# A decoder layer on one core: every step of the five queues set at a new place

## The reference

```python
# 1: x = LN(x + attn(x)); keys and values are weights
xn = LN(x) * ln_g + ln_b                      # 4 heads of 64
p = square(relu(einsum(xn, k)))               # k: 1024 x 64
y = x + einsum(p, v)
# 2: x = LN(x + xattn(x, ctx)); 16 heads of 16
attn = gamma * q @ k.T / 4 + delta * (ap * max(D, 0) + an * min(D, 0))
probs = softmax(attn); out = (probs @ v) @ Wo.T + bo     # D = clip(frac_k - frac_q)
# 3: x = LN(x + ffn(x)); the best of 8 experts by x @ gate_W.T + gate_b
inter = relu(x @ wi.T + wi_b + low_rank(expert)); out = inter @ wo.T + wo_b
```

## Time and profile before

| | us |
|---|---|
| median of 3 runs | 862.24 (862.21 to 862.75) |
| the profiled execution | 863.64 |
| its span, first to last instruction | 861.6 |
| PE busy | 827.0 (96%) |
| ACT busy | 698.4 (81%) |
| DVE busy | 679.7 (79%) |
| POOL busy | 599.0 (70%) |
| DMA queue q1, share of 16 engines | 26.1% |
| mean granted TensorE clock | 0.989 |

### The profile page before, as it was taken

One profiled execution on the slowest core, in us unless ns is written; L12 is line 12 of the kernel. 1 busy time (PEld: TensorE's weight loads), 2 busy tenths in 40 slices (PEclk: granted clock), 3 DMA queues, 4 the chain that ended last, 5 costly groups with the idle time before them and its releaser, 6 DMA issues.

```text
span 861.6 us, 23381 instructions
## 1 busy us (share of the span) xinstructions
PE 827.0 (96%) x8444; PEld 596.2 (69%) x8444; DVE 679.7 (79%) x2104; ACT 698.4 (81%) x1930; POOL 599.0 (70%) x782
## 2 busy tenths in 40 slices
PE   8989999999999999999999999999999999999897
PEld 6555557767676776767677676767767676677676
DVE  6788897878788787888878788787878877798943
ACT  4569998897988889798888979888897988887841
POOL 6478897777868687786868778686877867552411
PEclk9999999999999999999999999999999999999998
DMA  6242323222222322221232223123222312313100
GB/s 178 75 91 60 60 48 59 48 39 43 55 46 58 54 64 39 56 57 32 62 56 57 38 57 61 27 65 54 56 38 47 71 29 49 56 33 56 32 14 25
DMA packets 38149, 46.32 MB, mean 54 GB/s; under 512 B 10417, under 2 KB 27313, under 8 KB 38034
## 3 DMA queue, kind: packets, MB, share of 16 engines
q1 hardware_dynamic: 38034, 44.82, 26.1%
HBM read 15.42 MB, written 4.19 MB: 23 GB/s over the span
## 4 chain that ended last, share of the span: by engine, by line
PE 83%; ACT 7%; DVE 7%; issue 2%; POOL 1%; SPq 0%; DMA 0%; POOLq 0%; DVEq 0%; ACTq 0%
PE bank L308 12%; PE bank L295 12%; PE bank L503 11%; PE bank L256 10%; PE bank L421 8%; PE bank L435 6%; PE bank L405 4%; PE bank L381 4%; ACT R L655 2%; PE bank L328 2%; PE bank L362 2%; ACT P L711 2%; PE bank L342 2%; DVE T L940 2%; PE bank L513 2%
## 5 line engine op out<-in xcount | busy, mean ns | idle before, releaser
L1163 POOL TENSOR_TENSOR R<-R 128x512 f32<-128x512 f32 x236 | 247.3, 1050 | 84.9 <-ACT R L655 84.6
L711 ACT ACTIVATE P<-T,NM 128x256 f32<-128x256 f32 x512 | 257.5, 515 | 2.9 <-DVE NM L940 2.9
L1181 POOL TENSOR_SCALAR U<-DP,alph 128x512 f32<-128x512 f32 x256 | 180.3, 705 | 112.9 <-DVE NM L940 79.8
L931 DVE SCALAR_TENSOR_TENSOR bank<-DN,alph,bank 128x512 f32<-128x512 f32 x256 | 179.7, 747 | 53.5 <-PE bank L405 53.3
L940 DVE CUSTOM_DVE_ANT_0 T<-bank,U 128x256 f32<-128x256 f32 x512 | 186.4, 420 | 1.5 <-issue 0.6
L655 ACT ACTIVATE R<-bank 128x512 f32<-128x512 f32 x248 | 134.9, 601 | 61.8 <-PE bank L295 55.5
L633 ACT ACTIVATE STG<-bank 128x512 f32<-128x512 f32 x256 | 138.8, 600 | 8.5 <-PE bank L421 7.9
L308 PE MATMUL bank<-R,VS 128*32 128x512 f32 x992 | 120.6, 602 | 1.1 <-DVE X2b L884 0.9
L295 PE MATMUL bank<-SK,KH 64*128 64x512 f32 x480 | 108.5, 448 | 4.2 <-ACT R L655 1.4
L711 ACT ACTIVATION_READ_ACCUMULATOR P<-T,NM 128x1 f32 x512 | 105.5, 206 | 0.0
L421 PEld LDWEIGHTS bank<-ident,P 64*128 64x128 f32 x2048 | 75.4, 139 | 36.7 <-issue 13.6
(11 more groups left out here) (178 smaller groups left out, 1769.0 us busy)
## 6 DMA issues: line engine op xcount, KB each, us to landing
QS<-QK SPq DMA_DIRECT2D x384, 64.0 KB, 2.3
XG<-in_x SPq DMA_DIRECT2D x16, 256.0 KB, 2.8
CT<-in_ctxT SPq DMA_DIRECT2D x16, 256.0 KB, 3.2
out<-XO SPq DMA_DIRECT2D x15, 256.0 KB, 2.5
FK<-in_frac SPq DMA_DIRECT2D x16, 128.0 KB, 3.1
STG<-in_wiT SPq DMA_DIRECT2D x2, 512.0 KB, 4.4
STG<-in_woT SPq DMA_DIRECT2D x2, 512.0 KB, 4.4
STG<-in_kT SPq DMA_DIRECT2D x2, 256.0 KB, 4.1
```

The costliest lines, as they stand in the source:

```text
L711: eng.activation(P[n % NP][:, cs], T[n % NT][:, cs], ACT.Exp, bias=NM[:, n % 8, q:q + 1], scale=-1.0, accum_out=SU[n // 16 % 2][:, q, seat ...
L931: eng.scalar_tensor_tensor(out=L[:, :], in0=dn[:, :], scalar=alph[:, 16 + h:17 + h], in1=L[:, :], op0=ALU.mult, op1=ALU.add).then_inc(s_t1, 1)
L1163: eng.tensor_tensor(r, r, r, ALU.mult).then_inc(s_sqp, 1)
L1181: eng.tensor_scalar(U[n % NU][:, :], dp[:, :], alph[:, h:h + 1], 0.0, ALU.mult, ALU.add).then_inc(s_u, 1)
```

## The change

The functions that make the steps are not touched. What changes is the numbers at which the five GRID loops issue them: all `due` lines and all `g ==` lines, except a few. No step is added, dropped or given another operand; buffers and waits are written as before. Since `take` runs in the order of PE's queue, the banks of some steps change, and with them the step whose reader they wait for.

```diff
             for g in GRID:
-                if g == -4898:
+                if g == -3786:
                     pe.wait_ge(s_id, 1)
                     filler(15, pV)
...
-                for b, u in due(g, -4, 8, 74, early=27):
+                for b, u in due(g, 6, 8, 72, early=33, late=11):
                     logits(8 * b + u)
-                for b, u in due(g, 1308, 4, 33, early=-8, late=164):
+                for b, u in due(g, 1312, 4, 31, early=-16, late=118):
                     ffn_in(b, u)
-                for b, u in due(g, 1311, 4, 32, early=-8, late=227):
+                for b, u in due(g, 1320, 4, 29, early=-14, late=173):
                     low_rank(b, u)
-                for b, u in due(g, 1434, 8, 23, early=1, late=1136):
+                for b, u in due(g, 1432, 8, 24, late=1751):
                     ffn_out(b, u)
-                for b, _ in due(g, 767, early=-36, late=-21):
+                for b, _ in due(g, 767, early=-42, late=1):
                     rcT(b)
-                for b, u in due(g, 121, 8, 78, early=39, late=15):
+                for b, u in due(g, 121, 8, 78, early=50, late=40):
                     turn(8 * b + u)
-                for b, u in due(g, -946, 4, 151, early=-105):
+                for b, u in due(g, -951, 4, 154, early=4, late=-2):
                     av(b, u)
-                for b, u in due(g, 276, 4, 149, early=37, late=52):
+                for b, u in due(g, 276, 4, 147, early=29, late=63):
                     values(4 * b + u)
...
-                for b, _ in due(g, 861, early=45, late=-10):
+                for b, _ in due(g, 880, early=-13, late=-63):
                     op(b)
-                if g == -1061:
+                if g == -724:
                     bias_o()
-                for b, _ in due(g, -253, late=-8):
+                for b, _ in due(g, -264, early=-84, late=-2):
                     turned_over("x1T", b, X1, s_x1, 2 * b + 2, s_x1T)
-                for b, _ in due(g, -231, early=-900, late=37):
+                for b, _ in due(g, -220, early=-498, late=29):
                     kp(b)
...
-                for b, _ in due(g, 1236, early=-24, late=227):
+                for b, _ in due(g, 1265, early=5, late=190):
                     gsT(b)
-                for b, _ in due(g, 1289, early=-9, late=243):
+                for b, _ in due(g, 1308, early=-30, late=183):
                     uT(b)
-                for b, u in due(g, -1151, 8, 73, early=-255, late=4):
+                for b, u in due(g, -1151, 8, 73, early=-156, late=2):
                     scores(b, u)
...
-                for b, _ in due(g, 825, early=-7, late=103):
+                for b, _ in due(g, 771, early=-19, late=49):
                     aoh(b)
...
-                for b, _ in due(g, 681, early=-28, late=-104):
+                for b, _ in due(g, 570, early=68, late=139):
                     rc(b)
...
-                for b, _ in due(g, 2023, early=77, late=1318):
+                for b, _ in due(g, 2018, early=10, late=1718):
                     dve.wait_ge(d_o, 16 * b)
...
-                for b, u in due(g, 405, 4, 92, early=187, late=-230):
+                for b, u in due(g, 1090, 4, 56, early=-83, late=431):
                     restack(4 * b + u)
-                for b, _ in due(g, 2, start=1, late=-225):
+                for b, _ in due(g, 460, start=1, late=474):
                     load_f(b)
...
-                for b, _ in due(g, 2686, early=425, late=1586):
+                for b, _ in due(g, 3663, early=58, late=-615):
                     if b == NB - 1:
```

More of the change, by code:

```diff
@@ L604, in _ @@
                     turned_over("x1T", b, X1, s_x1, 2 * b + 2, s_x1T)
-                for b, _ in due(g, -231, early=-900, late=37):
+                for b, _ in due(g, -220, early=-498, late=29):
                     kp(b)
-                for b, _ in due(g, -208, early=18, late=29):
+                for b, _ in due(g, -216, early=12, late=52):
                     qp(b)
-                for b, _ in due(g, -138, early=128, late=-24):
+                for b, _ in due(g, -140, early=69, late=-17):
@@ L610, in _ @@
                     vp(b)
-                for b, _ in due(g, 1112, early=20, late=294):
+                for b, _ in due(g, 1121, early=13, late=85):
                     turned_over("x2T", b, X2, s_x2, 2 * b + 2, s_x2T)
-                for b, _ in due(g, 1163, early=14, late=300):
+                for b, _ in due(g, 1184, early=-32, late=209):
                     gate(b)
-                for b, _ in due(g, 1236, early=-24, late=227):
+                for b, _ in due(g, 1265, early=5, late=190):
@@ L624, in _ @@
                     xnT(1)
-                for b, _ in due(g, -1220, start=2, late=-2):
+                for b, _ in due(g, -1218, start=2, late=-15):
                     xnT(b)
@@ L767, in _ @@
             for g in GRID:
-                for b, u in due(g, 1289, 4, 36, early=-4, late=1653):
+                for b, u in due(g, 1301, 4, 31, early=-7, late=1544):
                     ih(b, u)
-                for b, _ in due(g, -374, early=-541):
+                for b, _ in due(g, -399, early=-2597, late=1):
                     x1(b)
-                for b, u in due(g, 29, 16, 37, early=20, late=21):
+                for b, u in due(g, 29, 16, 37, early=24, late=19):
                     exps(16 * b + u)
-                if g == -4264:
+                if g == -3916:
@@ L775, in _ @@
                     skh(0)
-                if g == -1560:
+                if g == -1133:
                     skh(1)
-                for b, _ in due(g, -1268, start=2, late=11):
+                for b, _ in due(g, -1259, start=2, late=4):
                     skh(b)
-                for b, _ in due(g, -498, early=-164, late=13):
+                for b, _ in due(g, -505, early=55, late=-8):
                     heads_out(b)
-                for b, u in due(g, 114, 8, 76, early=35, late=52):
+                for b, u in due(g, 111, 8, 78, early=31, late=60):
@@ L830, in _ @@
                     gs(b)
-                for b, _ in due(g, 1285, early=-43, late=-39):
+                for b, _ in due(g, 1273, early=-35, late=445):
                     ulh(b)
-                for b, u in due(g, -1160, 8, 70, early=-1041, late=6):
+                for b, u in due(g, -1155, 8, 69, early=-1077, late=6):
                     relu(b, 2 * u)
@@ L1079, in _ @@
                         centred("d", b, XO, X2b, s_xo)
-                if g == -2096:
+                if g == -1667:
                     dve.wait_ge(d_small, 160)
@@ L1116, in _ @@
                     cl(b)
-                for b, _ in due(g, -235, early=-14, late=64):
+                for b, _ in due(g, -268, early=-70, late=61):
                     low("x1T", b, X1L, X1H, s_x1h, s_x1l)
-                for b, _ in due(g, -206, early=-1396, late=77):
+                for b, _ in due(g, -240, early=-1260, late=59):
                     projected("kp", b, 2, 2, s_kh, s_kl)
-                for b, _ in due(g, -178, early=-22, late=58):
+                for b, _ in due(g, -205, early=17, late=59):
@@ L1122, in _ @@
                     projected("qp", b, 1, 0, s_qh, s_ql)
-                for b, _ in due(g, 1164, early=-41, late=-91):
+                for b, _ in due(g, 1145, early=-48, late=226):
                     low("x2T", b, X2L, X2H, s_x2h, s_x2l)
-                for b, _ in due(g, 1193, early=18, late=540):
+                for b, _ in due(g, 1196, early=-25, late=285):
                     gating(b)
-                for b, _ in due(g, 1282, early=15, late=961):
+                for b, _ in due(g, 1254, early=20, late=1376):
@@ L1128, in _ @@
                     ull(b)
-                for b, u in due(g, -1309, 16, 50, early=-674, late=107):
+                for b, u in due(g, -1213, 16, 43, early=-797, late=840):
                     if on_dve(b, u):
@@ L1225, in _ @@
                     plus(X1b[b % 2], X1, boB, s_x1b)
-                for b, _ in due(g, 1546, early=-342, late=131):
+                for b, _ in due(g, 1396, early=-61, late=260):
                     pool.wait_ge(s_x2, 2 * b + 2)
@@ L1231, in _ @@
                     plus(X2b, X2, woB, s_x2b)
-                for b, u in due(g, -1057, 16, 40, early=-591):
+                for b, u in due(g, -1112, 16, 36, early=-269, late=23):
                     if not on_dve(b, u):
```

200 lines of the change are left out of this document (100 added, 100 removed).

## The result

| | before | after |
|---|---|---|
| median of 18 runs each, us | 862.73 (860.43 to 864.40) | 856.90 (854.47 to 861.98) |
| ratio after to before, 95% interval | | 0.9934 (0.9921 to 0.9947) |
| the profiled execution | 863.64 | 857.19 |
| its span | 861.6 | 855.3 |
| mean granted TensorE clock | 0.989 | 0.990 |

The account below looks back on a forecast made before the run. TensorE was taken to bound the middle, ScalarE the ramp, latency the start, VectorE then latency the tail. From 863.64 us, block 4.8, head 3.9 and tail 1.8 gave 853.1, less 1.40 to the median: 851.7; range 846 to 859.

Parts of the forecast that it names:

- (a): TensorE, end of each steady block: logits 0 behind scores 7 and uT behind turn 7 gain 0.49 us a block.
- a wait on `exps` at `turn` 7: Sign of a wrong forecast, at the end of a steady block on TensorE; no size given.
- The wait that was to come back at `ffn_in`: End of each block: part of turn 7's wait returns at ffn_in 0, listed at 0.2 to 0.3 us in 12 blocks.
- (b): Steady block on TensorE: logits 7 ahead of turn 5 loses 0.06 us a block.
- (c): TensorE: values 3 ahead of logits 1, ffn_out 3 ahead of op; swaps booked at nothing, 0.03 us lost for the second.
- (d): Steady-block moves on the other engines, such as rc ahead of ull; each has 0.4 us or more to spare.
- The order of steps has a price: Steady block: TensorE loses time between one kind of step and the next, priced by distances between starts.
- Part 2: Head: x1T 5.2 us earlier, a quarter of the gain let go, first logits at 55.3, so 3.9 us gained.
- later than 58: Sign of a wrong forecast: logits 0 in the head starting after 58 us, where 55 to 56 was expected.
- rival B: Ramp: ScalarE, full from 100 to 150 us, swallows the head's gain; 855.6 us, chance 0.22.
- Part 3: Tail, from 750 us: low_rank's 1.05 us wait for ull goes and op 15 comes earlier; 1.8 us gained.
- Rival E: SyncE's queue: restack 1 behind load_f and the out DMA loses 6 us in 13 blocks; 940 us, chance 0.03.

Follow-up runs that it names:

- e5_noc: Kernel after with logits 1 ahead of values 3 again in the middle blocks; 858.28 us (one run).
- e7_rc: Kernel before with logits 0 behind scores 7, uT behind turn 7, values 3 ahead of logits 1, rc ahead of ull; 858.21 us (one run).
- e4_head: Kernel after with the first half-block's y1 ahead of the weights on VectorE; 854.97 us, ratio to before 0.9911.
- e10_head: Kernel before with only the head of the kernel after (steps due below 300 moved); 862.61 us, ratio to before 1.0008.
- e6_head: Kernel after with turn 5 ahead of logits 7, y1 ahead of the weights, and the way to the first logits cleared; 853.52 us, ratio to before 0.9898.
- e1_ut: Kernel before with only uT moved behind turn 7; 859.47 us (one run).
- e1_a: Kernel before with logits 0 of blocks 2 to 14 behind scores 7 and uT behind turn 7; 861.39 us, ratio to before 0.9988.
- e8_best: Kernel after with y1 ahead of the weights, turn 5 ahead of logits 7, and block 1's first logits ahead of scores 7; 853.07 us, ratio to before 0.9887.
- e3_nob: Kernel after with turn 5 ahead of logits 7 again in all blocks but first and last; 855.85 us, ratio to before 0.9912.

## Why the prediction was right, and where it was not

- **What bounds the middle, and (a) at `ffn_in` 0: right.** 4.65 became 4.19 (4.16 forecast). Its pieces too: `gsT` to `av` 0.20 (0.17), `scores` to `logits` 0.23 (0.24), `turn` 0.65 (0.64), `logits` to `turn` 0.41 where 0.34 was forecast. That 0.07 reads as a short wait for `exps`, by the 0.14 us that `turn` 7 keeps behind its end in each block; a wait on `exps` at `turn` 7 was one of my signs of being wrong, and it came, small. The wait that was to come back at `ffn_in` is there, as 0.28 from `uT` in place of 0.15, bound by the `relu` as forecast, but too short for the list of waits, where I had said it would show.
- **(b): right.** 0.07 against 0.06 us.
- **(c) and (d), "I book nothing" and "each has 0.4 us or more": wrong.** I compared each swap with its two neighbours on TensorE under the old timing. But (a) sends `uT` back and with it VectorE's chain from `ull` on, which ends at `logits` 1 and at `scores` 0. The swap of `values` 3 is worth 0.21 (e5_noc), `rc` ahead of `ull` 0.22 (e7_rc against e1_ac). Without them (a) gives 0.19, and with them 0.46. The change had both, and it also had (b) at 0.07 and some 0.06 that are left against e7_rc: 0.46 - 0.07 - 0.06 = 0.33, where 0.40 was forecast. The size came near for a wrong reason.
- **The order of steps has a price: right, but it is small.** If it were free, a block with the wait of 0.37 gone would take 49.64. e7_rc, with no wait listed, takes 49.55, so the new order is 0.09 us shorter. The formula N/2.4 + 2.5 ns between starts at the full clock, which the Trainium skill gives on its page TensorE: Matmul & The Clock Gate (Back-to-back issue gap), has no term for the neighbour, but the page keeps it to an isolated matmul and says that in a stream the weight load sets the spacing too. So it is no word for a free order, and no run here tells the weight load's part.
- **Part 2, the head: wrong in two steps.** First, `x1T` was to come 5.2 sooner: 3 from `otT`, and "all but 0.6" of the open 2.8 us ahead of `x1T`. `otT` came 2.2 sooner (38.20 and 36.04). The open 2.8 went, but 3.2 came on VectorE where 0.6 was allowed: `y1` started 2.45 us behind the end of `otT` (39.12 and 36.67), as the two weights ahead of it took 2.06 us each where they took 1.22 before, and `centred` b took 1.49 and not 0.74. e4_head confirms it: with `y1` ahead of them `x1T` comes at 42.70 although its `otT` was 1.2 later. Second, and decisive, the gain was to pass through the ramp, less a quarter. It does not (e10_head: 0.9 us at `logits` 0 at most, none in the time; e6_head: 3.1 us there, 0.9 at the next). The first `logits` at 59.11 also met a sign of being wrong, "later than 58". That was rival B, to which I gave 0.22, and its 855.6 is nearer to 856.9 than my 851.7. Its argument, that ScalarE is full from 100 to 150 and what starts sooner "only queues sooner", is not shown: most of the gain of e6_head is gone at `logits` 1, at 62 us already, and what holds the ramp, ScalarE, VectorE or another, was not tested.
- **Part 3, the tail: right in size, by luck in part.** 2.1 us in the profile against 1.8, and the wait of `low_rank` went as said, with 0.68 of its 0.95 us left at `op` 15. But the same steps behind `gsT` 12 take 119.6 us in the kernel after, with 13.7 us at the lower level of the clock, and 117.1 in e4_head, with 6.8. Against the 121.7 us of the kernel before that is a gain of 2.1 or of 4.5, by the profile that is taken.
- **Rival E: out.** No wait for QS in the middle of either profile.

## What to carry to other kernels

When a queue is bound by one engine, price a swap by the new timing, not the old: list every step that the main edit delays on the other engines, follow each to the next place where the bound engine waits for it, and see whether one of the "free" swaps stands there. Test the main edit alone and in halves; here one half was better than the whole. A head start at one milestone is not a gain: follow a second milestone, one step of work further, before it enters the sum.

## What the runs showed of the hardware

**The clock of TensorE moves the time by as much as the edits do.** The traces show two levels, 2.4 GHz (granted 1.00) and 1.2 GHz (0.50), and spells at the lower one that fall differently in each kernel, all ahead of 110 us and behind 770. There TensorE has idle gaps: it is busy for some 44 of 50 us from 60 to 110 in the kernels of the table of the head, 87.32 of 100 in the last row below. The columns are those of the earlier trace rows; first the kernel before, then the kernel after, then e1_ut, which has no such spell in the tail:

```profile
64.50:67.90 3.40, 3.40 (x21) 0.74 (x18) 3.12 (x10) 2.06 (x6) 3.40 (x4) 0.58 0.63 98
```

```profile
807.90:818.10 10.20, 9.15 (x85) 5.73 (x78) 6.30 (x26) 7.53 (x24) 2.31 (x4) 0.53 0.01 2
```

```profile
750.00:850.00 100.00, 87.32 (x924) 73.33 (x923) 76.19 (x241) 66.30 (x194) 34.00 (x53) 1.00 0.16 32
```

From `gsT` 12 to the end the kernel before, with 10.2 us at the lower level, takes 121.7 us, and e1_ut, whose tail differs by the place of `uT` alone, takes 119.2 with none: 2.5 us. In the 18 runs of the kernel after the span is 852.6 to 854.6 where the mean clock was 0.993 or 0.994, 855.0 to 856.6 at 0.990 to 0.992, and 860.0 at 0.986. In e1_a the mean clock was 0.988 to 0.990 in all ten runs, beside 0.989 to 0.994 in the kernel before: its middle is some 2.1 us shorter (11 times 0.19), its time only 0.8. In its profile `gsT` 1 comes at 187.64, 1.3 us later than before, with two spells between 60 and 110 us where before has one. So a new order can also bring or take such spells, and a few tenths of a per cent of the time say nothing without the clock beside them.

**VectorE and GpSimd hold each other up.** The subtraction of a weight (128x1024) on VectorE occurs 56 times in the fourteen profiles. The 40 that began while GpSimd was idle took 1.21 to 1.23 us, also where GpSimd started during them. Sixteen began inside an instruction of GpSimd. Fourteen of these took as long as was left of GpSimd's instruction, and 1.07 to 1.09 us more: 2.05 or 2.06 with 0.98 left, 1.75 with 0.66 left (e8_best), 1.46 with 0.38 left (e3_nob). The other two took 1.21 and 1.22; there GpSimd's instruction, of a kind that takes 1.05 on the mean, took 2.12 (e4_head) and 2.94 (e3_nob), so it looks as if GpSimd was the one held up. Here are the two GpSimd instructions inside which the weights at 35.15 and 37.13 of the kernel after began:

```profile
35.00 1.13 POOL L1163 TENSOR_TENSOR R<-R 128x512 f32<-128x512 f32 x1 [6.86 <-ACT R L655]
...
36.78 1.33 POOL L1163 TENSOR_TENSOR R<-R 128x512 f32<-128x512 f32 x1 [0.65 <-ACT R L655]
```

The Trainium skill says on its page SBUF — State Buffer (Terms, shared port pair) that the two share a pair of ports which is locked for a whole instruction, and that the loser blocks fully. Blocked until GpSimd's end (36.13 and 38.11) the two would end at 37.35 and 39.33; they end at 37.21 and 39.19, 0.14 sooner. So the rows agree with a block much more than with a shared speed. In the kernel before the same weights happened to meet an idle GpSimd; the difference, 1.7 us for the two, is lost ahead of `y1`.
